# Perceiver block on one core: the start of self-attention prepared inside the last two tiles of cross attention

## What is computed

```python
x = x + xattn(layernorm(x), ctx_512, Wq, Wkv, Wo)       # 16 heads of 32, 257 keys of width 256 per batch row
x = x + attn(layernorm(x), wq, w_down, wk_up, wv_up, wo)
x = x + ffn(layernorm(x), Wr, W1, W2, W3)               # 8 experts, top 2, hidden 768

def attn(x):                                            # causal by pages of 128, so here all 32 tokens see each other
    q = rope(x @ wq)
    lat = x @ w_down                                    # 512 -> 256, "the latents"
    k, v = rope(lat @ wk_up), lat @ wv_up
    return softmax(q k^T / sqrt(32)) v @ wo
```

## Time and profile before

| | us |
|---|---|
| median of 3 runs | 1525.81 (1523.08 to 1526.02) |
| time of the profiled execution | 1520.73 |
| its span, first to last instruction | 1519.0 |
| mean granted clock of PE | 0.98 |
| PE busy | 1442.4 (95%) |
| DVE, ACT, POOL busy | 1084.9, 809.2, 542.2 |

### The profile page before, as it was taken

One profiled execution on the slowest core, in us unless ns is written; L12 is line 12 of the kernel. 1 busy time (PEld: TensorE's weight loads), 2 busy tenths in 40 slices (PEclk: granted clock), 3 DMA queues, 4 the chain that ended last, 5 costly groups with the idle time before them and its releaser, 6 DMA issues. The chain is left out here.

```text
span 1519.0 us, 39483 instructions
## 1 busy us (share of the span) xinstructions
PE 1442.4 (95%) x14944; PEld 1288.8 (85%) x14944; DVE 1084.9 (71%) x1939; ACT 809.2 (53%) x1527; POOL 542.2 (36%) x816
## 2 busy tenths in 40 slices
PE   7999999999999999987999998799999999999996
PEld 6888888888888888775778786688999999999995
DVE  3667677777776777754657687787877878788783
ACT  4666666666666666644433434235555555555551
POOL 1222222222222222224866877443333333333332
PEclk9999999999999999998999999799999999999998
DMA  6301110000001001100001114169877878787771
GB/s 234 127 22 30 30 28 23 26 28 28 24 26 28 21 28 29 29 2 1 30 30 37 38 37 156 56 203 318 280 261 236 299 251 271 257 269 255 248 246 43
DMA packets 130734, 174.11 MB, mean 115 GB/s; under 512 B 16953, under 2 KB 89337, under 8 KB 130626
## 3 DMA queue, kind: packets, MB, share of 16 engines
q1 hardware_dynamic: 120242, 145.56, 29.5%
q0 software_dynamic: 10384, 27.05, 4.9%
HBM read 157.18 MB, written 19.06 MB: 116 GB/s over the span
## 5 line engine op out<-in xcount | busy, mean ns | idle before, releaser
L2204 DVE TENSOR_TENSOR split<-raw,split 128x1024 fp32r<-128x1024 f32 x202 | 240.0, 1220 | 6.3 <-ACT split L2145 4.9
L52 PE MATMUL bank<-split_xT,split 128*128 128x256 f32 x768 | 217.3, 283 | 0.6 <-DVE split L2204 0.6
L53 PE MATMUL bank<-split_xT,split 128*128 128x256 f32 x768 | 216.3, 282 | 0.0
L54 PE MATMUL bank<-split_xT,split 128*128 128x256 f32 x768 | 216.3, 282 | 0.0
L2145 ACT CAST split<-raw 128x1024 fp32r<-128x1024 f32 x202 | 203.1, 1048 | 3.6 <-DMA raw<-in_L_ffn_W_dram 3.6
L591 ACT ACTIVATE Pr<-xa_s,nmax 128x257 f32<-128x257 f32 x256 | 118.9, 473 | 125.0 <-DVE nmax L687 124.9
L2165 ACT ACTIVATE sl<-bank 128x256 f32<-128x256 f32 x117 | 44.9, 385 | 242.6 <-PE bank L54 242.6
L52 PE MATMUL xa_s<-split 128*128 128x258 f32 x512 | 150.6, 294 | 1.9 <-DVE split L619 1.9
L52 PEld LDWEIGHTS bank<-split_xT,split 128*128 128x128 f32 x768 | 145.8, 190 | 6.7 <-issue 2.6
L53 PEld LDWEIGHTS bank<-split_xT,split 128*128 128x128 f32 x768 | 145.8, 190 | 3.2
L53 PE MATMUL xa_s<-split 128*128 128x258 f32 x512 | 145.7, 285 | 0.0
(11 more groups left out here) (311 smaller groups left out, 3925.9 us busy)
## 6 DMA issues: line engine op xcount, KB each, us to landing
raw<-in_L_ffn_W_dram SPq DMA_DIRECT2D x207, 512.0 KB, 6.1
raw<-in_ctx_dram SPq DMA_DIRECT2D x64, 256.0 KB, 2.6
out_dram<-x_res SPq DMA_DIRECT2D x16, 256.0 KB
xs<-xn SPq DMA_DIRECT2D x16, 256.0 KB, 2.7
x_res<-in_x_dram SPq DMA_DIRECT2D x1, 3584.0 KB, 18.7
VL<-v_last_rows SPq DMA_DIRECT2D x128, 2.0 KB, 1.5
raw_o<-in_L_xattn_Wo_dram SPq DMA_DIRECT2D x1, 1024.0 KB, 6.3
raw_q<-in_L_xattn_Wq_dram SPq DMA_DIRECT2D x1, 1024.0 KB, 9.4
```

The costliest lines, as they stand in the source:

```text
L52: pe.matmul(out, lh, rh, start=start, stop=False)
L53: pe.matmul(out, ll, rh, start=False, stop=False)
L54: return pe.matmul(out, lh, rl, start=False, stop=stop)
L2204: vW.done(dve.tensor_tensor(lo, raw, hi.bitcast(F32), ALU.subtract), f"p{c}{q}")
```

## The change

Five things.

1. Layer norm of self-attention's tiles 0 and 1 is made in cross attention's tiles 14 and 15, by the same helpers with i + 2 = 16 and 17 (`rows_of` takes the remainder by 16). Tile 0 is turned and copied there too (`turn_x`, `x_out` in tile 14), so that its normalised, turned rows lie in `xg[:, 1]` when self-attention begins; tile 1's normalised rows lie in `xg[:, 0]`. Self-attention's `xn` and `xnT` are now these two buffers.
2. The splits of Wq and Wk go to cross attention: the high parts on ACT behind the last `pt_hi`, the low parts on DVE behind `last_rows` and behind `ot_lo` of tile 15. For that, scratch and Wo have changed places in `held.w13`. The split of Wv and of Wo stay in self-attention.
3. In the very last step DVE makes `last_weights` before `pt_lo`, not behind it.
4. Self-attention begins on PE with `latents(0)`, then `turn(1)`, then the queries.
5. `Steps` can start counting at a later tile (`first`), and POOL no longer waits for the weights by itself.

```diff
+        def rows_of(i):
+            return x_res[:, i % n_tile if isinstance(i, int) else i, :]
...
-        QK_hi, QK_lo = held.parts(held.w13[0], 0, 2, C)
+        QK_hi, QK_lo = held.parts(held.w13[1], 0, 2, C)
...
-                        if j == 2 and more:
+                        if j == 2 and not last:
                             need(pe, v_OP, i)
                             turn_x(pe, i + 2)
...
-                        if j == 2 and more:
+                        if j == 2 and not last:
                             x_out(act, i + 2)
...
                 by_pair(act, tile)
+                weights.wait(act)
+                act.wait_ge(pe_S, 4 * s_end)
+                weights.high(act, 0)
+                weights.high(act, 1)
                 u_out(s_end - 1, BT - 1)
                 ot_hi(n_tile - 1)
...
-                        if j == 2 and more:
+                        if j == 2:
                             normalise(dve, i + 2)
...
-                        if j == 1 and more:
+                        if j == 1:
                             if first:
                                 dve.wait_ge(x_rest, 16)
                             statistics(dve, i + 2)
                         if j == 0 and not first:
                             ot_lo(i - 1)
+                        if last and j == BT - 1:
+                            last_weights(i)
                         pt_lo(s)
-                        if j == BT - 1:
+                        if j == BT - 1 and not last:
                             last_weights(i)
...
                 last_rows(n_tile - 1)
+                dve.wait_ge(pe_U, s_end)
+                weights.low(dve, 0)
                 ot_lo(n_tile - 1)
+                weights.low(dve, 1)
                 add_residual(n_tile - 1)
...
+    def high(self, act, n):
+        raw, hi, _lo = self.split[n]
+        act.copy(*(t[:].rearrange("p k c -> p (k c)") for t in (hi, raw))).then_inc(self.hi_done, 1)
+
+    def low(self, dve, n):
+        raw, hi, lo = (t[:].rearrange("p k c -> p (k c)") for t in self.split[n])
+        dve.wait_ge(self.hi_done, n + 1)
+        dve.tensor_tensor(lo, raw, hi.bitcast(F32), ALU.subtract).then_inc(self.lo_done, 1)
...
-                turn(0)
                 latents(0)
                 turn(1)
...
-                normalise(0)
-                w.wait(act)
-                turned(0)
-                normalise(1)
                 high(0)
-                weights_hi(0)
+                w.high(act, 2)
                 latents(0)
                 turned(1)
-                weights_hi(1)
-                weights_hi(2)
                 queries(0)
...
-                statistics(vN, gN, 0, st6, mv)
-                w.wait(dve)
-                statistics(vN, gN, 1, st6, mv)
                 low(0)
-                weights_lo(0)
                 latents(0)
-                weights_lo(1)
-                weights_lo(2)
                 statistics(vN, gN, 2, st6, mv)
+                w.low(dve, 2)
                 low(1)
                 latents(1)
-                weights_lo(3)
+                w.low(dve, 3)
```

More of the change, by code:

```diff
@@ L85, in cross_attention @@
 def cross_attention(nc, x_in, ctx_in, Wq, Wkv, Wo, x_res, ident, vlast_dram, spare,
-                    spare_x, held, ahead, beside):
+                    spare_x, held, weights, beside):
     n_tile = x_res.shape[1]
@@ L114, in cross_attention @@
         WqT = sb("WqT", [P, KC, C])
-        WoT_hi, WoT_lo = (held.parts(held.w13[1], n, 1, C)[0] for n in range(2))
+        WoT_hi, WoT_lo = (held.parts(held.w13[0], n, 1, C)[0] for n in range(2))
         Wk = sb("Wk", [P, NQ, L])
@@ L164, in normalise @@
             dve.wait_ge(g_ln, i + 1)
[L165 removed]
+            dve.tensor_scalar(xn, rows_of(i), mv[:, 0:1], rstd[:], ALU.subtract, ALU.mult
                               ).then_inc(v_ln, 1)
@@ L368, in tile @@
                     if first:
-                        ahead(sp)
+                        weights.load(sp)
                 by_pair(sp, tile)
@@ L753, with __init__ @@
 class Steps:
-    def __init__(self, sem, names):
-        self.sem, self.names, self.next = sem, names.split(), 0
+    def __init__(self, sem, names, first=0):
+        self.sem, self.names, self.next, self.first = sem, names.split(), 0, first
     def done(self, op, name):
@@ L764, in wait @@
     def wait(self, eng, i, name):
-        need(eng, self.sem, len(self.names) * i + self.names.index(name) + 1)
+        if isinstance(i, int) and i < self.first:
+            return
+        need(eng, self.sem, len(self.names) * (i - self.first) + self.names.index(name) + 1)
 def statistics(dve, steps, i, suffix, x, st6, mv, waiter):
@@ L785, with __init__ @@
 class SelfAttentionWeights:
-    def __init__(self, nc, ctx, later, wq, w_down, wk_up, wv_up, wo, Wr, rope):
+    def __init__(self, nc, ctx, later, held, wq, w_down, wk_up, wv_up, wo, Wr, rope):
         def sb(name, shape):
@@ L809, in __init__ @@
         self.loads.append((self.rope[:], rope.rearrange("p (a d) -> p a d", a=2)))
+        width = wq.shape[1]
+        self.split = [(self.q, *(held.parts(held.w13[1], n, 1, width)[0] for n in range(2))), (self.k, held.w2_hi, held.w2_lo)]
+        self.hi_done, self.lo_done = (ctx.enter_context(nc.semaphore(n)) for n in ("sa_w_hi", "sa_w_lo"))
+    def high(self, act, n):
[5 more added lines that the diff above has]
+        dve.tensor_tensor(lo, raw, hi.bitcast(F32), ALU.subtract).then_inc(self.lo_done, 1)
     def load(self, sp):
@@ L841, in sb, with steps @@
             return ctx.enter_context(nc.sbuf_tensor(name, shape, dt))
-        def steps(name, names):
-            return Steps(ctx.enter_context(nc.semaphore(name)), names)
+        def steps(name, names, first=0):
+            return Steps(ctx.enter_context(nc.semaphore(name)), names, first)
         Wdown, Wg, rope_t = w.down, w.router, w.rope
-        Wq_hi, Wq_lo = (held.parts(held.w13[1], n, 1, C)[0] for n in range(2))
-        Wk_hi, Wk_lo = held.w2_hi, held.w2_lo
+        (_q, Wq_hi, Wq_lo), (_k, Wk_hi, Wk_lo) = w.split
         Wv_hi, Wv_lo = sb("sa_wv_hi", [P, KL, C], F32R), sb("sa_wv_lo", [P, KL, C], F32R)
         Wo_hi, Wo_lo = sb("sa_wo_hi", [P, KC, C], F32R), sb("sa_wo_lo", [P, KC, C], F32R)
-        split_weights = [(w.q, Wq_hi, Wq_lo), (w.k, Wk_hi, Wk_lo), (w.v, Wv_hi, Wv_lo), (w.o, Wo_hi, Wo_lo)]
+        w.split += [(w.v, Wv_hi, Wv_lo), (w.o, Wo_hi, Wo_lo)]
         below = sb("below", [P, P])
@@ L1219, in _ @@
                 turned(2)
-                weights_hi(3)
+                w.high(act, 3)
                 queries(1)
```

36 lines of the change are left out of this document (14 added, 22 removed).

## The result

| | before | after |
|---|---|---|
| median, us | 1525.81 (1521.25 to 1526.22, 5 runs) | 1515.54 (1513.09 to 1519.22, 5 runs) |
| profiled execution / its span | 1520.73 / 1519.0 | 1518.23 / 1516.2 |
| PE, DVE, ACT, POOL busy | 1442.4, 1084.9, 809.2, 542.2 | 1443.2, 1086.6, 807.6, 546.1 |
| mean granted clock | 0.98 | 0.98 |

The ratio is 0.9941 (95% interval 0.9918 to 0.9963), 5.6 to 12.5 us less. The two medians differ by 10.3, the two profiled executions by 2.5 only: the trace has to say which of the two is the change.

What follows compares the result with a forecast made beforehand. PE was taken to set self-attention's pace, so its waits at the seam between the attentions could be gained. 8.6 + 1.1 - 0.5 + 1.0 = 10.2 us off 1525.8 gave 1515.6, range 1511.3 to 1519.6.

Steps and rivals of the forecast that it cites:

- scores(0), from B: Self-attention's first scores, counted from the block's start: 18.3 us in place of 26.92, gain 8.6, bounds 6.3 and 10.8.
- last weights: Cross attention's last step: made before `pt_lo`, they let `gather_z` start earlier; gain 1.1 us, bounds 0 and 1.1.
- tiles 14 and 15: Cross attention's last tiles: PE's four added transposes cost 0.5 us, bounds 0 and 1.1; DVE's added work costs 0.
- splits in the tail: Cross attention's tail: the Wq and Wk splits on ACT and DVE are hidden by waits, cost 0.
- clock: `gather_z` at cross attention's end: full clock may be back earlier; 1.0 us taken between 0 and 2.6.
- The start of self-attention: Block's start: latents run at once, queries begin 2.4 us behind it, formerly 10.25; gain 7.85, bounds 5.5 and 8.1.
- The full clock over the latents: First latents of self-attention: full clock taken, 1.95 us; at half clock 3.60, queries 4.7 behind the block's start.
- The wait before `scores(0)`: Self-attention's first tile: DVE's Wo split holds POOL's second key-rotation product; start at 18.3 us, wait some 2.2; unheld 16.1.
- a sign of being wrong: Cross attention's tiles 14 and 15: more than 0.6 us lost there would make the forecast wrong.
- The rivals: Whole kernel: part of the gain lost (0.14), more comes out (0.07), no change (0.05), slower (0.04).
- a new wait at the block's start: Seam between the attentions: part of it comes back as a wait, gain 4 to 6.5 us; chance 0.14.
- "Slower" by the clock of the loop: Self-attention loop: further half-clock stretches cost about 1.7 us each, more than six lose the 10.2; chance 0.04.

Runs made afterwards that it cites:

- before_third: The old kernel, unchanged, profiled a third time; 1524.39 us.
- after_third: The changed kernel, unchanged, timed again beside the old kernel on another chip; 1516.79 us, ratio 0.9945.
- wo_late: Changed kernel with DVE's split of Wo's low part put behind the turn of tile 0's heads; 1509.60 us, old kernel beside it 1520.77.
- both_again: Second run of the changed kernel with POOL's last z split held for the last weights and DVE's Wo split behind tile 0's head turn; 1515.56 us, ratio 0.9937.
- before_again: The old kernel, unchanged, profiled a second time; 1522.73 us.
- splits_only: Changed kernel with norm and turn of tiles 0 and 1 back at self-attention's start, Wq and Wk splits kept in cross attention; 1521.01 us, ratio 0.9993.

## Why the prediction was right, step by step

The forecast, 1515.6 for a measured 1515.54, is closer than its working deserves: that it fell within 0.1 is luck. The two timings of the changed kernel together (0.9941 +- 0.0023 and 0.9945 +- 0.0015, weighted by their widths) give 0.9944 +- 0.0012, so 8.6 +- 1.9 us, where the sum had 10.2. By terms:

| term | predicted | measured |
|---|---|---|
| scores(0), from B | 8.6 (B + 18.3) | 9.0 (B + 17.95 from 26.95; 9.5 from 27.45) |
| last weights | 1.1 | 0.29 |
| tiles 14 and 15 | -0.5 | -0.43 (turns); -1.1 in the mean with the falls of the clock |
| splits in the tail | 0 | 0 |
| clock | 1.0 | none found |
| sum | 10.2 | 8.2 to 9.4 |

- **The start of self-attention: right.** Queries came at B + 2.25, 0.15 from the forecast. The full clock over the latents, which was a choice, held in all nine profiles of kernels that begin with them (2.02 each).
- **The wait before `scores(0)`: right, in its cause too.** Of the part that speaks of a held rotation, both numbers came out: 3.76 beside DVE's split, a wait of 2.03 for some 2.2. Without the split it is 1.80 and B + 16.01, and the prediction had B + 16.1, set by PE. The Trainium skill, GPSIMD Engine Reference, Specifications (contention with a DVE instruction of two SBUF inputs), names such a sharing; by 3.76 beside the split and 1.80 without it, the trace agrees.
- **`last_weights` earlier: the step that failed in size.** It said "It takes about 0.7", from a place where POOL was idle, and so "the hole of 1.37 before `pt_lo`" would hold it. At the new place POOL's split of z begins with it, and it takes 2.29: over the hole by 0.9, by which `pt_lo` comes later. The prediction weighed this very sharing for the split of Wo and did not ask it of the other DVE work that it moved. POOL's row at this place was not read at all. With POOL held the term is 0.86 of 1.1, and then POOL's own split of z comes last: it ends 0.33 behind `pt_lo` there (674.03 and 673.70).
- **The clock: wrong.** The 1.0 was a mean between two ends, with no mechanism. `gather_z` takes 3.1, 4.3 to 4.6 or 5.5 from its start to the copy of `U`, and each of the three lengths occurs in the old kernel and in the changed one: the old has 5.5, 4.34, 3.08, 5.49, the changed 5.50, 4.61, 3.08. The windows of the third profiles of both show full clock there (columns as in rows 1), first `before_third`, then `after_third`:

```profile
674.00:677.00 3.00, 3.00 (x14) 2.51 (x15) 1.29 (x2) 0.00 (x0) 0.00 (x0) 1.00 0.00 0
```

```profile
674.00:677.00 3.00, 2.61 (x11) 2.18 (x12) 1.49 (x3) 1.33 (x2) 0.00 (x0) 1.00 0.00 0
```

  Set side by side by that length, from D to `scores(0)` the changed kernel is 9.3 (5.5 each) and 9.6 (3.08 each) ahead. The Trainium skill, TensorE: Matmul & The Clock Gate, What's actually happening, says that how many matmuls run cold (at the low clock) varies between runs of one kernel. The prediction could not show it; these rows agree, with 3.1 to 5.5 us for the same twelve products. No term for the change comes out of them.
- **Tiles 14 and 15: right in the work, silent on the clock.** The turn moves the next instruction on PE by 0.43. DVE's added work is hidden: it waits 1.04 ahead of `pt_lo` where it waited 2.06, 0.65 ahead of the reciprocal where it waited 1.10. From PE's turn of `Pr` at 606 to 607 us (tile 13) to D it is 62.95 to 62.98 in three of the old profiles and 63.38 to 63.41 in `after_third`, `wo_late` and `both_again`: 0.43 more. But with the fall of the clock in tile 14 it is 64.5 (`before_again`, and `splits_only`, which has no norm there) and 64.9 to 65.0 (the other six with the norm), so a fall costs 1.5. By the first pair of profiles 1.99 was lost, over the 0.6 that the prediction gave as a sign of being wrong; 1.5 of it is this fall, which the old kernel can have too. It came in six of nine profiles with the norm and in two of five without. Whether the change makes it more frequent stays open.
- **The splits in the tail: right.** ACT's stood 4.56 ahead of the asked-for copy, and even in `after_third`, where the gather ran at full clock, ACT still waited 2.14 for it.
- **The rivals.** Of the 10.2 some 1.8 did not come (0.8 of the last weights, 1.0 of the clock), by terms that were priced too high and not by a new wait at the block's start, and 0.4 to 0.9 came beyond the forecast at `scores(0)`. "Slower" by the clock of the loop is out: the granted clock is 0.95 over 704 to 984 in all three profiles of the changed kernel and 0.95 to 0.96 in the four of the old.

## What to carry to other kernels

When work is moved, read the row of the engine that shares something with it at the new place, for each piece moved, the small ones above all: here four DVE instructions of 0.78 us in sum took 2.29 because POOL had begun a 0.61 us cast 0.04 before the first and a 1.3 us subtraction 0.08 before the third. Where two gates stand ahead of the same work, expect little from opening the one that would open first anyway (1.5 of 8.0 here, against 5.5 for the later one), and price the pair together. Follow a gain to the next common point before calling it one: 1.94 at `scores(0)` was gone at `scores(1)`. And take a term for the clock only where the change touches what PE does ahead of the stretch in a way a row shows; the profiled executions of the old kernel differed by up to 4.5 us in the span and 6.9 us behind the seam, more than most steps that were argued.

## What the runs showed of the hardware

- DVE and POOL did not slow each other down in proportion: the one that began first kept its time, and the other ended behind it, by 0.03 to 0.7. DVE's split of Wo took 2.29 and POOL's two products 3.76 instead of 1.79 (the second began behind the split and ended 0.7 after it); POOL's subtraction took 1.30, and DVE's 128x128 product 1.36 instead of 0.28, its 128x16 cast 0.60 instead of 0.18 beside POOL's cast of 0.61. The Trainium skill, Trainium Architecture — The Big Picture, What this means for kernel authors, calls the port pair that DVE and GpSimd share "an exclusive lock (not a bandwidth split)"; by these rows the trace agrees. So the price of a short instruction is what is left of the long one, nearly five times its own time here.
- The 128x16 cast has one input. What brought it into conflict was not tried.
- The old kernel itself stands at 1520.77 (17 runs), 1524.89 (11) and 1525.81 (5) on three occasions; only ratios taken side by side compare two kernels at this size.
- From DVE's residual to the first instruction of the next block it is 1.19 to 1.20 us in all fourteen profiles.
